# Two expert blocks started before the routing is known, and half blocks computed with the rows stationary

## The reference, cut to what matters

```
logits = x @ gate_w + gate_b                       # x: 4096 x 256, 8 experts
top_w, top_idx = top_k(softmax(logits), 2);  top_w = top_w / sum(top_w)
h     = silu(x @ w1[e]) * (x @ w3[e])              # w1, w3: 8 x 256 x 1024
out_e = h @ w2[e]                                  # w2: 8 x 1024 x 256
x = x + tanh(g_ffn[1]) * sum over the two experts of top_w * out_e
```

## Time and profile before

| | us |
|---|---|
| median of 3 runs (2076.02 to 2078.50) | 2077.61 |
| the profiled execution, its own time | 2078.52 |
| its span, from the first to the last instruction | 2076.8 |
| PE busy | 1896.8 (91%) |
| DVE busy | 1550.3 (75%) |
| ACT busy | 1149.3 (55%) |
| POOL busy | 928.8 (45%) |
| mean granted TensorE clock, as a share of full speed | 0.969 |

### The profile page before, as it was taken

How to read it: one execution, slowest core, us unless ns; L and a number is a source line. 1 busy time by engine, 2 the same in 40 slices (tenths; PEclk the granted TensorE clock), 3 DMA queues, 4 the chain that set the end, 5 groups by cost and what they waited for, 6 DMA issues and landing times. The chain is left out here.

```text
span 2076.8 us, 35512 instructions
## 1 busy us (share of the span) xinstructions
PE 1896.8 (91%) x12100; PEld 1340.9 (65%) x12100; DVE 1550.3 (75%) x3240; ACT 1149.3 (55%) x2414; POOL 928.8 (45%) x672
## 2 busy tenths in 40 slices
PE   5899999986889999998999999939999999999998
PEld 3566677664543434343434343439999999999998
DVE  7999999982566777676767778547877776777775
ACT  2456666655346555555555555516665565656664
POOL 6999999981633335253434341112222231222222
PEclk8899999997999999999999999969999999999999
DMA  5222222300515142424242441036767666666662
GB/s 175 113 92 113 110 93 113 123 21 10 126 46 122 47 107 67 107 69 108 80 98 87 95 113 44 32 97 228 238 228 239 226 226 210 219 227 230 232 229 89
DMA packets 138569, 271.47 MB, mean 131 GB/s; under 512 B 13243, under 2 KB 90255, under 8 KB 132498
## 3 DMA queue, kind: packets, MB, share of 16 engines
q1 hardware_dynamic: 127916, 243.63, 37.4%
q0 software_dynamic: 9952, 25.25, 3.3%
q10 hardware_dynamic: 518, 0.27, 0.0%
HBM read 200.12 MB, written 70.47 MB: 130 GB/s over the span
## 5 line engine op out<-in xcount | busy, mean ns | idle before, releaser
L1472 DVE CUSTOM_DVE_ANT_0 x_dump<-x_ps,x_bias_q 128x512 bf16<-128x512 f32 x512 | 353.2, 690 | 103.7 <-PE x_ps L1156 90.7
L1341 ACT ACTIVATE x_PT<-x_ps 128x512 f32<-128x512 f32 x512 | 292.7, 603 | 230.0 <-PE x_ps L1171 226.5
L2017 ACT ACTIVATE X<-m_ps 128x256 f32<-128x256 f32 (+1 forms) x312 | 114.1, 366 | 221.7 <-PE m_ps L1949 218.2
L1156 PE MATMUL x_ps<-x_KS,x_QS 96*128 96x512 bf16 x512 | 199.1, 389 | 23.2 <-DVE x_mx L1472 22.5
L1915 POOL DMA_INDIRECT out_dram<-e_y,e_label x71 | 71.4, 1006 | 320.5 <-DVE e_y L2077 310.7
L1170 PE MATMUL x_ps<-x_bias_k,x_ident_b 128*128 128x512 bf16 x512 | 196.7, 384 | 2.1 <-DMA x_QS<-x_rows 1.0
L1171 PE MATMUL x_ps<-x_QS,x_KS 98*128 98x512 bf16 x512 | 196.6, 384 | 0.0
L1949 PE MATMUL m_ps<-e_x_lo,m_hi 128*128 128x256 f32 (+1 forms) x640 | 180.5, 282 | 5.9 <-issue 4.4
L1949 PE MATMUL m_ps<-e_x_hi,m_lo 128*128 128x256 f32 (+1 forms) x640 | 180.4, 282 | 0.0
L1949 PE MATMUL m_ps<-e_x_hi,m_hi 128*128 128x256 f32 (+1 forms) x640 | 180.4, 282 | 0.0
L2059 DVE TENSOR_TENSOR X<-X,m_ps 128x256 f32<-128x256 f32 (+1 forms) x312 | 114.3, 394 | 85.9 <-ACT X L2017 81.1
(11 more groups left out here) (332 smaller groups left out, 5417.5 us busy)
## 6 DMA issues: line engine op xcount, KB each, us to landing
m_raw<-in_L_ffn_w_dram SPq DMA_DIRECT2D x117, 1024.0 KB, 5.0
expert_in<-a_blank SPq DMA_DIRECT2D x34, 1032.0 KB, 4.3
parts<-x_part SPq DMA_DIRECT2D x24, 512.0 KB, 3.8
m_x<-expert_in SPq DMA_DIRECT2D x32, 258.0 KB, 5.1
next_mask_k<-in_maskT_dram SPq DMA_DIRECT2D x32, 256.0 KB, 2.7
next_mask_q<-in_mask_dram SPq DMA_DIRECT2D x29, 256.0 KB, 2.9
x_KS<-parts SPq DMA_DIRECT2D x16, 384.0 KB, 11.2
x_QS<-parts SPq DMA_DIRECT2D x8, 576.0 KB, 6.7
```

The source lines that it names most:

```text
L1156: pe.matmul(ps_max[m % 2], QS[b % 2][0:HROWS, h, q * P:(q + 1) * P], KS[b % 2][0:HROWS, h, :], start=True, stop=True).then_inc(s1_ps, 1)
L1341: act.activation(PT[unit % 2][:, k, :], ps_st[e % 3], ACT.Exp, scale=DH ** -0.5).then_inc(exp_done, 1)
L1472: dve.tensor_tensor_reduce(out=dump[:, :], in0=ps_max[m % 2], in1=bias_q[b % 2][:, q, :], scale=1.0, scalar=NEG, op0=ALU.add, op1=ALU.max, ...
L2017: act.activation(silu[f % 2][:, 0:wide], ps_h[f % 4][:, 0:wide], ACT.Silu).then_inc(silu_done, 1)
```

## The change

The routing program block goes. Its work moves to the head of the slots' program block.

- A new step, `gate_largest`, in `cross_attention` finds, from the counts of the first seven batches, the expert with the most rows: 8 chained small VectorE instructions, at gate step 14 of the seventh batch. Slots 0 and 1 are then the first two full blocks of that expert (`KNOWN`); the table holds the other 37, and four instructions are added to its chain to leave these two out.
- SP starts with the rows of slots 0 and 1 and the weights of slot 0, without waiting for the table or the scatters; then the weights of slot 1; then it waits for both.
- POOL copies the second coefficients itself, between its two groups of scatters.
- PE transposes slot 0's rows first, and runs the idle matmuls once w1's high part is there. On VectorE the table's chain stands ahead of `x_low` and the low parts of slot 0.
- A half slot runs `hidden_by_row`: the rows' 128 x 128 pieces are stationary and 512 columns of the weights move, 24 matmuls in place of 96. Silu and the product work on 512 columns at a time, two of each in place of eight. The product then has the hidden features along the free dimension, so PE transposes it back (`turn_gated`, 8 transposes into the PSUM banks that are free by then), and ACT and DVE take the high and low parts of g from there, two of each in place of four.
- Around a half slot the weight parts are spread otherwise: the slot before it also does w1 for the slot after it (after `x_high` on ACT, before `add_y` on DVE); the half slot does w3 first of all, and w2 after the rows' parts.

```diff
-        with ExitStack() as route:            # the routing program block, whole
...
             def _(sp):
-                load_weights(sp, 0, 1)
-                for q in range(2, ROUND):
+                for q in range(KNOWN):
+                    load_rows(sp, 0, q)
+                for q in range(KNOWN):
+                    load_weights(sp, 0, q)
+                sp.wait_ge(blocks_known, 1)
+                sp.wait_ge(routing.scattered, 16 * NT * TOPK)
+                for q in range(KNOWN, ROUND):
                     load(0, q)
...
+                for k in range(TOPK):
+                    if k:
+                        pool.wait_ge(routing.scattered, 16 * (TOPK * TPB * B + TPB))
+                        pool.tensor_copy(routing.XN[:, :, D], routing.coef[:, 1, :]).then_inc(routing.labelled, 1)
+                    pool.wait_ge(routing.labelled, TOPK * B + k + 1)
+                    for j in range(TPB):
+                        scatter_rows(pool, routing, xs, k, j)
...
+                def hidden_by_row(p):
+                    for h in range(2):
+                        for n in range(2):
+                            for c in range(KC):
+                                mm = three_passes(ps_h[2 * h + n], [x[p][:, c, 0:P] for x in (x_hi, x_lo)],
+                                                  [w[p][n][:, c, h * HALF_FF:(h + 1) * HALF_FF] for w in (w_hi, w_lo)], c == 0, c == KC - 1)
+                        mm.then_inc(h_ps, FC // 2)
+
+                def turn_gated(j):
+                    for h in range(2):
+                        pe.wait_ge(gated_done, FC * j + FC // 2 * (h + 1))
+                        for f in range(FC // 2):
+                            mm = pe.transpose(ps_h[h][:, f * P:(f + 1) * P], wide_gated[h][:, f * P:(f + 1) * P], ident_f[:, :])
+                        mm.then_inc(g_turned, 1)
+
                 def project(i, q):
+                    if tiles == 1:
+                        turn_gated(j)
...
                 turn(0, 0)
+                pe.wait_ge(hi_done[0], 1)
+                for _ in range(16):
+                    pe.matmul(ps[:, 7, 0:P], ident_f[:, :], ident_f[:, :], start=True, stop=True)
...
+                def hidden_by_row(i, q):                                       # on ACT
+                    high_part(act, j + 1, 1 - p, 1)
+                    act.wait_ge(gated_done, FC * j)
+                    for h in range(2):
+                        act.wait_ge(h_ps, FC * j + FC // 2 * (h + 1))
+                        act.activation(wide_silu[h], ps_h[2 * h], ACT.Silu).then_inc(silu_done, FC // 2)
+                    for h in range(2):
+                        act.wait_ge(g_turned, 2 * (len(HALVES) * i + halves_before(q)) + h + 1)
+                        act.activation(g_hi[:, 4 * h:4 * h + 4, 0:P], ps_h[h].rearrange("p (f n) -> p f n", n=P), ACT.Copy)
...
+                def following_parts(i, q):
+                    x_high(i, q + 1)
+                    if tiles_in(q) == 1:
+                        high_part(act, j + 1, 1 - p, 2)
+                    if tiles_in(q + 1) == 1:
+                        high_part(act, j + 2, p, 0)
...
+                def gate_by_row(j, p):                                         # on DVE
+                    low_part(dve, j + 1, 1 - p, 1)
+                    for h in range(2):
+                        dve.wait_ge(silu_done, FC * j + FC // 2 * (h + 1))
+                        dve.tensor_tensor(wide_gated[h], wide_silu[h], ps_h[2 * h + 1], ALU.mult).then_inc(gated_done, FC // 2)
+                    for h in range(2):
+                        dve.wait_ge(g_high, FC // 2 * j + FC // 4 * (h + 1))
+                        dve.tensor_tensor(g_lo[:, 4 * h:4 * h + 4, 0:P], ps_h[h].rearrange("p (f n) -> p f n", n=P),
+                                          g_hi[:, 4 * h:4 * h + 4, 0:P].bitcast(F32), ALU.subtract).then_inc(g_parts, FC // 4)
...
                     low_part(dve, at_slot(i, q) + 1, 1 - q % 2, 2)
+                    if tiles_in(q + 1) == 1:
+                        low_part(dve, at_slot(i, q) + 2, q % 2, 0)
                     add_y(i, q)
```

More of the change, by code:

```diff
@@ L25 @@
 NBLK = FULL + HALF
+KNOWN = 2
+LATER = FULL - KNOWN
 ROUND = 10
@@ L1626, in _ @@
                         part(step_of(unit, step))
+                if step_of(unit, 14) == BATCH - 2:
+                    gate_largest(BATCH - 2)
                 b = step_of(unit, 17)
@@ L1860, in experts @@
             gated = [X[:, 2 * n + 2:2 * n + 4, :] for n in range(2)]
+            wide_gated = [gated[n].rearrange("p t d -> p (t d)") for n in range(2)]
+            wide_silu = [X[:, 2 * n + 6:2 * n + 8, :].rearrange("p t d -> p (t d)") for n in range(2)]
             g_hi, g_lo = sb("g_hi", [P, FC, BLK], F32R), sb("g_lo", [P, FC, BLK], F32R)
@@ L2083, in slot, with do @@
                     low_part(dve, at_slot(i, q) + 1, 1 - q % 2, 2)
+                    if tiles_in(q + 1) == 1:
+                        low_part(dve, at_slot(i, q) + 2, q % 2, 0)
                     add_y(i, q)
+                steps = Steps(dve, chain)
+                def do(ins):
+                    steps.done(ins)
+                    steps.wait()
+                dve.wait_ge(iotas, 5)
+                do(dve.tensor_copy(flat[:, :], flat_i[:, :]))
+                do(dve.tensor_tensor(total[:, :], routing.ends_at[0:1, :], routing.region[0:1, :], ALU.subtract))
@@ new lines, in _ @@
+                c, n, now = 0, 1, size
+                while n < NE:
+                    do(dve.tensor_copy(upto[c][:, :, 0:n], now[:, :, 0:n]))
+                    do(dve.tensor_tensor(upto[c][:, :, n:NE], now[:, :, n:NE], now[:, :, 0:NE - n], ALU.add))
+                    c, n, now = 1 - c, 2 * n, upto[c]
+                do(dve.tensor_scalar(over[:, :], now[:, 0, NE - 1:NE], float(LATER * BLK), None, ALU.subtract))
+                do(dve.tensor_scalar(more[:, :], over[:, :], 0.0, None, ALU.max))
@@ new lines, in _ @@
+                do(dve.tensor_scalar(less[:, :], over[:, :], -0.5, None, ALU.mult))
+                do(dve.tensor_copy(limit[:, 0, :], where[:, 0, :]))
+                do(dve.tensor_scalar(limit[:, 1, :], where[:, 1, :], less[:, 0:1], None, ALU.add))
+                do(dve.tensor_scalar(less[:, :], less[:, :], 0.0, None, ALU.max))
+                do(dve.tensor_scalar(limit[:, 1, LATER:], where[:, 1, LATER:], less[:, 0:1], more[:, 0:1], ALU.add, ALU.subtract))
+                do(dve.tensor_scalar(weight[:, 0, :], size[:, 0, :], -1.0, None, ALU.mult))
@@ new lines, in _ @@
+                do(dve.tensor_tensor(taken[:, :, :, :], past[:, :, :, :], wide(weight), ALU.mult))
+                do(dve.tensor_reduce(left[:, :, :], taken[:, :, :, :], AX.X, ALU.add))
+                do(dve.tensor_tensor(left[:, 0, :], left[:, 0, :], where[:, 0, :], ALU.add))
+                do(dve.tensor_scalar(left[:, 1, :], left[:, 1, :], size[:, 0, 0:1], None, ALU.add))
+                do(dve.scalar_tensor_tensor(out=number[:, :, :], in0=n_past[:, :, :], scalar=float(T), in1=left[:, :, :], op0=ALU.mult, op1=ALU.add))
```

196 lines of the change are left out of this document (96 added, 100 removed).

## The result

The changed kernel is slower: 2094.9 us median of 10 runs (2081.6 to 2097.7) against 2076.4 of the kernel before beside them, ratio 1.0076 (95% interval 1.0054 to 1.0098). 2050 was forecast, 2038 to 2065 as the range, 0.04 for slower. The profiled execution has 2096.5, its span 2094.7.

What follows compares the result with a forecast made beforehand. TensorE's stream was taken to bound the slots, one chain the hand-over. Gains of 14 (hand-over) and 14 (half slots), less 0.5, make 27.5 off the profiled 2078.5: 2051, so 2050 as the median; range 2038 to 2065.

Steps and rivals of the forecast that it cites:

- Hand-over: Between attention and slot 0: table and barrier leave the chain to the first loads; 14.1 us gained, 14 taken.
- rival (c): Hand-over gains nothing or half, loads held by scatters and rows: 2064 or 2057; sign: w1 usable over 8 us after issue; chance 0.09.
- What `gate_largest` costs: Eight small VectorE instructions at the end of a unit of the attention: between 0 and 1.7 us, 0.5 taken.
- Half slot by itself: One half slot, hidden through project: 11.4 us instead of 13.98, gain 2.6, with 2.0 of idle PE in it.
- what is queued behind: Half slot's `add_y` fetch at 15.2 us, wanted at 13.3; VectorE late into the next slot, PE hardly stopped; 0.6 us charged.
- The bound of -0.5 per half slot: Worst gain for one half slot: the fetch comes 2.5 us later and that goes to PE in full.
- 14 was summed: The half slots' total gain: 2.0 us for each of the seven.
- (a): TensorE's clock falls in half slots after short pauses: 2062 with three or four and slot 0's start, 2074 with all; chance 0.23.
- (b): Half slot bound by PE alone, VectorE's work falling better than lined up: gain 4.6 each, time 2032; chance 0.09.
- (d): In half slots, fp32r operands stream 512 columns at half rate, spacing over 0.4 us: slower, time 2088; chance 0.04.
- the last of my signs of being wrong: `add_y` waits over 3 us for its fetch after each half slot, with PE stopped in the full slot behind.

Runs made afterwards that it cites:

- hold_only: The changed kernel with only the load of w3 held on SP until the half slot's fetch has landed: 2039.7 us, 0.9829 of the kernel before.
- busy_wait: The changed kernel with 18 identity matmuls on TensorE where it waits for the product in the slot behind each half slot: 2110.9 us, ratio 1.0173.
- add_first: The changed kernel with `add_y` of the slot before a half slot ahead of the additional low part of w1: 2087.7 us, ratio 1.0061.
- padded: The changed kernel with 10 identity matmuls behind the last matmul of each half slot: 2111.8 us, ratio 1.0158.

## Why the prediction was wrong

- **Hand-over**: right in size, 13.6 of 14.1, but in part because two misses offset each other. w1 was usable only 8.1 us after its issue instead of 5.4, which I had named as rival (c)'s sign, but w3 came 2.6 behind it instead of 5.5, and TensorE waited for w3's low part (1398.2). What `gate_largest` costs, 0.5 in my sum, isn't shown: it is lost in the wandering of the attention's end (last point).
- **Half slot by itself**: right, 11.2 of 11.4. Spacing 0.233 us at 512 columns (0.225 taken), and 11.16 - 10.18 = 1.0 us of idle TensorE in it, by the stretch's row, where I gave 2.0. My reason, that the weight loads set the spacing because they were busy all the time, isn't shown: they are busy in 17.40 of 17.40 us of the full slot too, where the matmuls have 256 columns.
- **The step that failed** is "what is queued behind": "15.2 instead of 13.3 wanted", "I charge 0.6". `add_y` came 20.3 us after the half slot's start. The fetch was issued at 12.9, not 9.5: one scatter issue took 2.18 instead of 1.0, and from the end of the last scatter's issue to the fetch it took 5.43 where I had taken 2.94 from the earlier trace rows, a moment in which the loads of w1 and w3 had not yet been issued. The fetch then took 7.4 where I had 5.65. TensorE could go on until 17.0 us after the half slot's start, as I had said; the product came at 21. The bound of -0.5 per half slot assumed a fetch 2.5 us later; it was 5.1, and the stop's clock came on top.
- What I had left out: I moved low parts ahead on VectorE's list but not what they release. Each low part frees a buffer, and SP loads 1 MB into it. Before, w1's and w3's loads were issued from 7.4 us into the half slot on, when the scatters had landed (the fetch was issued at 7.9). Now w2's, w1's and w3's are issued at 0.1, 2.5 and 5.3 us, all beside the scatters (w2's at 0.1 was there before as well). hold_only shows this to be the cause: with w3's load held until the fetch has landed, 12.9 us into the half slot (it was issued at 11.4 before the change), the rest of the change stands as forecast. In its profile the slots take 645.6 us, 14.5 less than before, where 14 was summed, and the hand-over 1389.1 - 1369.4 = 19.7, 13.1 less.
- **Rivals**: (a) the clock did not fall in the half slots in spite of the short pauses; it fell behind the stops in the slots behind them, six of 4.1 to 5.3 us and one of 2.2. (b) is refuted by the idle time, (d) by the spacing. (c): see above. What happened stood only as the last of my signs of being wrong and, as a late fetch, in the bound of -0.5. It was a rival with a mechanism, a place and a price above that bound, and I gave it no chance.
- Not settled: the attention's end wanders between profiles of equal code (it ends from 1367.9 to 1379.5, and slot 0 starts from 1387.8 to 1399.5, in the kernels with the new hand-over), and hold_only's attention ended at 1369.4 against 1375.85 before. So some 6 to 9 of the 36 us between the medians of these two I can't place. Nor did I measure how the early load of w1 weighs, or how much of the gain is w2's load, held behind w3's.

## What to carry to other kernels

An instruction that is moved takes along the transfers that it releases: put each of them on the time line with its new issue time, and look what latency-bound transfer it now meets. A read-modify-write through DRAM has a period of its own; compare its turn with the shortest slot and with the mean of the slots, and take its landing times from moments with the load that it will have. A wait on a load that isn't urgent (two lines here) can be worth more than the faster arithmetic.

## What the runs showed of the hardware

- A POOL indirect DMA took 0.99 to 1.45 us to issue in the 76 of 128 cases (changed kernel, 1400 to 2030) in which no low part ran on VectorE beside it. Of the 52 beside one, the 26 that shared up to 1.0 us with it took 1.00 to 1.52, and the 26 that shared over 1.2 us took 2.17 to 3.13. The Trainium skill, "GPSIMD Engine Reference", section "8. Key points", says that GpSimd shares its SBUF interfaces with VectorE and names VectorE instructions with two SBUF inputs as contenders; the low part is one (w and its high part), and the trace agrees. A chain that meets a low part in this way is 1.2 to 2.1 us longer.
- Lateness feeds itself. Where `add_y` waits for its fetch, the low part behind it starts together with the next scatters and lengthens their issue (1489.49: 2.85 us), and its load meets their landing. In busy_wait the turn stayed at 18.9 to 19.9 us for four turns on end (slots 4 to 8). It fits the spread: 2074 to 2115 in add_first, 2038 to 2045 in hold_only. That it is this alone was not tried.
- TensorE's clock fell to 1.2 GHz behind each of the six stops of 4.1 to 5.3 us in the slots behind half slots of the changed kernel, and not at the two pauses of 0.7 and 0.3 us at most in each half slot. In between, the length of the stop alone does not decide: in hold_only it fell behind a stop of 1.8 us (granted 0.57 from 1978 to 1982), in padded it stayed at 1.00 behind one of 2.2 us (1850.3 to 1856).
